# A recommendation tower on one core: each gathered group of embeddings is transposed in two pieces of 256 batch columns, the first one unit ahead of the second

## What is computed

```python
e = jnp.stack([tbl_0[ids[:, 0]], ..., tbl_39[ids[:, 39]]], axis=1)        # (512, 40, 32)
z = jnp.einsum('bpd,pde,bpe->bp', e[:, iidx, :], bilinear_matrices, e[:, jidx, :])   # (512, 780)
h = jnp.concatenate([z, dense_ctx], axis=1)                                # + 16 dense
h = jnp.maximum(h @ W_top1 + b_top1, 0.0)                                  # 796 -> 512
h = jnp.maximum(h @ W_top2 + b_top2, 0.0)                                  # 512 -> 256
y = h @ W_top3                                                             # 256 -> 1
```

## Time and profile before

| | us |
|---|---|
| median of 3 runs | 174.76 |
| lowest and highest of them | 174.19, 174.95 |
| the profiled execution, whole | 174.02 |
| its span in the profile | 172.2 |
| TensorE busy | 166.6 (97%) |
| VectorE busy | 145.4 (84%) |
| GpSimd busy | 115.1 (67%) |
| ScalarE busy | 43.6 (25%) |

### The profile page before, as it was taken

The page is one execution under the profiler, slowest core; times in us unless marked ns, Lnnn a source line. Parts: engine busy times, 40 slices in busy tenths (PEclk is TensorE's granted clock), DMA queues, the critical chain, the costliest instruction groups (busy, mean ns, idle before and its releaser), DMA issues.

```text
span 172.2 us, 4016 instructions
## 1 busy us (share of the span) xinstructions
PE 166.6 (97%) x1710; PEld 54.0 (31%) x1710; DVE 145.4 (84%) x144; ACT 43.6 (25%) x58; POOL 115.1 (67%) x119
## 2 busy tenths in 40 slices
PE   6999899999999999999999999999999999999993
PEld 2344344313333323332233333323233232232330
DVE  1799899889899998998999998999999999892600
ACT  2389994040101211102111201112100121110503
POOL 3777777777777777777777777777799995112000
PEclk9999999999999999999999999999999999999999
DMA  5999156986998720000006610001001650000000
GB/s 133 370 404 382 30 151 195 314 260 203 317 371 264 227 62 11 15 15 16 11 13 182 188 42 15 15 11 19 11 6 47 154 168 4 2 0 4 0 0 0
DMA packets 12699, 19.95 MB, mean 116 GB/s; under 512 B 3829, under 2 KB 6777, under 8 KB 12553
## 3 DMA queue, kind: packets, MB, share of 16 engines
q1 hardware_dynamic: 9144, 18.03, 31.9%
q0 software_dynamic: 3072, 1.58, 5.1%
q10 hardware_dynamic: 464, 0.09, 0.3%
HBM read 11.82 MB, written 0.00 MB: 69 GB/s over the span
## 4 chain that ended last, share of the span: by engine, by line
PE 85%; ACT 4%; DMA 4%; issue 2%; DVE 1%; SPq 1%
PE y_ps L559 33%; PE z_ps L630 27%; PE t_ps L530 11%; PE y_ps L530 7%; DMA table<-hot_tables 4%; PE y_ps L573 3%; PE t_ps L573 3%; ACT plane L414 2%; PE z_ps L573 1%; DVE prod L513 1%; ACT z_t L424 1%; SPq L356 1%; ACT xt L433 0%; ACT hot_id L471 0%; ACT xt L434 0%
## 5 line engine op out<-in xcount | busy, mean ns | idle before, releaser
L513 DVE TENSOR_TENSOR prod<-y_ps,xt 128x1024 f32<-128x1024 f32 x98 | 114.8, 1219 | 8.0 <-PE y_ps L559 3.5
L339 POOL DMA_INDIRECT x_rows<-rows,row x96 | 92.1, 960 | 29.2 <-issue 29.0
L559 PE MATMUL y_ps<-xt,m_sb 32*128 32x512 f32 x392 | 59.5, 640 | 0.0
L630 PE MATMUL z_ps<-prod,sel 128*32 128x512 f32 x392 | 52.2, 604 | 0.6 <-issue 0.4
L530 PE MATMUL t_ps<-z_t,table 128*32 128x256 f32 x352 | 27.1, 379 | 0.0
L488 DVE TENSOR_SCALAR hot<-hot_id,number 128x2048 bf16<-128x2048 int16 x34 | 22.8, 746 | 4.6 <-DMA hot_id<-hot_ids 4.1
L559 PEld LDWEIGHTS y_ps<-xt,m_sb 32*128 32x128 f32 x392 | 17.8, 182 | 22.6 <-DVE prod L513 13.4
L530 PEld LDWEIGHTS t_ps<-z_t,table 128*32 128x32 f32 x352 | 11.4, 110 | 26.3 <-issue 26.3
L630 PEld LDWEIGHTS z_ps<-prod,sel 128*32 128x32 f32 x392 | 7.8, 108 | 37.4 <-DVE prod L513 22.3
L573 PE MATMUL y_ps<-hot,plane 128*32 128x512 bf16 x200 | 15.1, 379 | 0.7 <-ACT plane L414 0.7
L347 POOL TENSOR_TENSOR hot_id<-x_rows,hot_id 128x512 f32<-128x512 f32 x6 | 7.6, 1272 | 9.5 <-ACT x_rows L457 9.5
(11 more groups left out here) (39 smaller groups left out, 62.3 us busy)
## 6 DMA issues: line engine op xcount, KB each, us to landing
xt<-xt SPq DMA_DIRECT2D x18, 192.0 KB, 2.5
xt<-xt SPq DMA_DIRECT2D x17, 128.0 KB, 2.4
hot_id<-hot_ids SPq DMA_DIRECT2D x4, 512.0 KB, 6.2
xt<-xt SPq DMA_DIRECT2D x32, 64.0 KB, 2.0
x_rows<-rows,row POOLq DMA_INDIRECT x96, 2.3
table<-hot_tables SPq DMA_DIRECT2D x2, 640.0 KB, 8.9
table<-w SPq DMA_DIRECT2D x1, 1280.0 KB
table<-hot_tables SPq DMA_DIRECT2D x2, 512.0 KB, 5.4
```

Of the source, the lines that this page charges most:

```text
L339: pool.indirect_dma_start(out=x_rows[:, g, c, :], out_offset=None, in_=rows, in_offset=bass.IndirectOffsetOnAxis(ap=row[:, n:n + 1], axis= ...
L513: nc.vector.tensor_tensor(prod[:, k % PROD_UNITS, 2 * half:2 * half + 2, :], y_ps[:, 2 * slot:2 * slot + 2, :], partners[half], ALU.mult). ...
L559: last = nc.tensor.matmul(y_ps[:, 2 * slot + place(t, u, s) % 2, :], m_sb[rows, k, :], xt[rows, moving(t, u, s), :], start=True, stop=True)
L630: last = nc.tensor.matmul(z_ps[s * DIM:(s + 1) * DIM, :], window, prod[:, k % PROD_UNITS, place(*UNIT[k], s), :], start=first, stop=(k == ...
```

## The change

The one transposition of a gathered group becomes two, of chunks 0 to 7 (columns 0 to 255) and chunks 8 to 15 (columns 256 to 511). `AFTER["turn"]` now has a unit for each piece. The first group's two pieces stand side by side ahead of unit 1; the others have the second piece where the whole turn stood, and the first piece ahead of the unit before. The wait for the gather stands ahead of the first piece, and is for all 16 chunks as before. Waits on `turned` count two for each group.

```diff
+TURN_PIECES = 2
...
-    "turn": [1, 8, 17, 23, 31, 39],
+    "turn": [(1, 1), (7, 8), (16, 17), (22, 23), (30, 31), (38, 39)],
...
-            engine.wait_ge(turned, GATHER_POS.index(t) + 1)
+            engine.wait_ge(turned, TURN_PIECES * (GATHER_POS.index(t) + 1))
...
-                            act.wait_ge(turned, part_free[b])
+                            act.wait_ge(turned, TURN_PIECES * part_free[b])
...
-                for g in [g for g, before in enumerate(AFTER["turn"]) if before == k]:
+                for g, piece in [(g, n) for g, units in enumerate(AFTER["turn"]) for n in range(TURN_PIECES) if units[n] == k]:
                     t = GATHER_POS[g]
-                    dve.wait_ge(gathered[g], 16 * CHUNKS)
-                    nc.vector.transpose(xt[:, t, :], x_rows[:, g, :, :].rearrange("p c d -> p (c d)")).then_inc(turned, 1)
+                    if piece == 0:
+                        dve.wait_ge(gathered[g], 16 * CHUNKS)
+                    part = slice(piece * CHUNKS // TURN_PIECES, (piece + 1) * CHUNKS // TURN_PIECES)
+                    nc.vector.transpose(xt[:, t, part.start * DIM:part.stop * DIM],
+                                        x_rows[:, g, part, :].rearrange("p c d -> p (c d)")).then_inc(turned, 1)
```

## The result

The changed kernel takes 177.34 us in the median of 6 runs, beside 174.78 of the kernel before: a ratio of 1.0132, 95% interval 1.0098 to 1.0165. The forecast was 176.8 us, range 175.5 to 178.0. The profiled execution took 177.31 us, with a span of 175.5, 3.3 more than before. Ratios here come from the executions of both kernels with the slow ones left out, and aren't quotients of the medians (which give 1.0146 here); where the two differ enough to matter, both are given.

What follows compares the result with a forecast made beforehand. TensorE was taken to bound the kernel, with VectorE's turns holding it up. A loss of 2.38 us at units 7 and 8 less 0.4 won elsewhere gave +2.0, so 176.8 us on the 174.76 median; range 175.5 to 178.0.

Steps and rivals of the forecast that it cites:

- What bounds the kernel: TensorE is busy 97% of the span; VectorE matters only where it holds TensorE up, about 0.46 us a turn.
- The gather isn't there one unit early: Group 4's gather lands at about 50.1 us, but the first piece ahead of unit 7 could start at 47.53.
- The working by steps: At units 7 to 10, the first piece's wait delays products and matmuls until unit 10 starts 2.38 us late.
- the sum: 2.38 us lost at units 7 and 8, less 0.4 won at the last four turns: +2.0 us.
- rival B: TensorE pauses 1.6 us in unit 8 and its clock falls: 2.9 us more, 179.7 us; chance 0.04.
- three signs that I had named for a wrong prediction: VectorE doesn't idle ahead of unit 7, a piece costs far from 440 ns, or matmuls behind the pause are slow.
- Unit 9's second half: It waits for unit 8's first product, which ends at 54.46, and starts at 54.51, 0.26 us late.
- The other four turns: Turns ahead of units 17, 23, 31 and 39: two pieces win 0.10 us each, -0.4 us together.
- The 0.05 us that goes free: Lateness of a product behind a turn that TensorE doesn't feel, some 0.05 us, counted against the pieces' cost.
- Rival A: Group 4's gather lands in time, at 46.0, so VectorE doesn't wait: -0.6 us, 174.2 us; chance 0.10.
- Rival C: A piece costs as much as a whole turn, 703 ns: about +2.5 us over the forecast, 179.3 us; chance 0.04.

Runs made afterwards that it cites:

- the kernel with the busy pause: The changed kernel with extra, overwritten matmuls filling TensorE's pause ahead of the second half of unit 8: 176.46 us, ratio 1.0123.
- the repeat: The changed kernel timed again, unedited, beside the kernel before: 177.47 us, ratio 1.0132.

## Why the prediction was right, and where its sizes were off

**What bounds the kernel**, and that a turn costs TensorE some 0.46 us: right. Small pieces, which fit into the spare time, take 0.40 of it away in each of four turns; from unit 7 to unit 48 that trace is 1.6 us shorter, and 2.15 with all five. The medians moved by more, 2.2 and 2.75 us. The kernel with only the loads moved shows the same surplus, some 0.5 us, over its trace, so part of it is probably that the traced execution of the kernel before was one of its better ones.

**The gather isn't there one unit early**: right, by the idle VectorE of 2.73 us (2.5 forecast) and by the kernel with only the wait moved. That SP's loads are the cause holds for about 3 us of the lateness; the other 1.2 have no cause that a run shows.

**The working by steps**, for the profiled executions (+3.3 where the sum gave +2.0):
- The first piece started at 50.35, not 50.12, and half of unit 8 at 51.96 (51.75 forecast): +0.2.
- Unit 9 starts at 56.09. With 2.50 us behind 51.96 it would have been 54.46: 1.6 us of slow clock, which I had kept out of the sum as **rival B with a chance of 0.04**. This is the term that was mis-sized. It came together with the forecast's mechanism, in ten of twelve executions. One of the three signs that I had named for a wrong prediction came true with it: the matmuls behind the pause are slow (1.73 and 1.94 us). Unit 10 starts at 58.59 and not near 57.0. My argument was that the longest pause before was 0.54 us and that work went on around it; no row showed how long a pause the clock bears, and I took that silence for a low chance. Its price of 2.9 us was too high: 1.6 in the trace, 1.4 net of what it covered, 1.0 between medians. That price came from the 14 first matmuls at 0.42 us each. The profile gives a granted clock of 1.00 for them too, so that they ran at the 1.2 GHz level was read from their length alone.
- Unit 9's second half, forecast 0.26 late, wasn't: the slow stretch covered it. With the clock kept up it is 0.24 late (1.38 us for 1.14, in the kernel with the busy pause). From 54.63 to 58.59, unit 10 is 3.96 late; 2.38 + 0.2 + 1.6 - 0.26 = 3.9.
- The other four turns gave back 0.66 us (3.95 late at unit 17, 3.29 at unit 48), not 0.4. The piece itself was right: 428 ns beside 439, and 0.36 and 0.46 us from start to start beside 0.36 and 0.48. The 0.05 us that goes free was counted once, but it goes free in each of the two units: 0.82 - 0.44 - 0.10 is 0.28 lost, and the matmuls of units 23 and 24 take 1.18 and 1.38 us, 0.28 over twice 1.14.

The medians differ by 2.6 us, beside 2.0 forecast, and that the two are so close is partly luck. The forecast added 0.74 us, by which the traced execution of the kernel before stood under its median. The changed kernel's traced execution (177.31) stands at its median (177.34), so those 0.74 us weren't there, and they made up for half of the slow clock. The two executions at full clock, 175.41 and 175.58 us, lie 1.2 us and more under the forecast; one of them is below its range.

**Rival A** (gather in time) was priced wrong. At -0.6 it left out its own consequence: the prediction called the later gathers close and had them in time because of the delay at unit 8. Without that delay an early piece waits for its own gather, group 7's in one trace (1.17 us) and group 8's in another (0.87). The kernel with the loads behind the gather came to 0.9996, not 0.995. Of the kernels with two pieces only the one with shorter waits (a semaphore for each piece) is faster than before.

**Rival C** is out: 428 ns for 256 columns, 297 for 128, 703 for 512.

## What to carry to other kernels

When an instruction is moved forward, move its wait in thought first: look in the trace for when the data landed, not for when the work was done, and for what stands between the new place and the old. Work that is cut into pieces to fit into another engine's spare time needs a wait that is cut too; here the pieces lost 1.3% with one wait for all the data and won 0.5% (two pieces) or 1.4% (four) with a wait each. Four pieces under one wait weren't tried, so how much of the 1.4% is the size and how much the waits isn't shown. Give a repair its control in the old kernel: moving the loads alone won 0.3%. A stall of TensorE is to be priced twice, for its length and for the clock behind it, here 1.8 and 1.6 us.

## What was unexpected of the hardware

Pauses of TensorE of 1.81 us, and of 2.24 in the repeat's trace, both of them behind about 1 us in which only half of a unit's matmuls ran, were followed by some 3 us at a granted clock of 0.50. One execution in six of each series kept 1.00 or 0.998, with a pause that no trace shows. With work in the pause, down to 0.34 us of idle time, the clock stayed in five of five. The gather's last chunk landed more than 6 us behind its issue at about 43.7 while the DMA engines were some 100% busy, where the median of all 96 is 2.3 us. With SP's loads held back and the DMA engines 6% to 12% busy from 44.0 to 47.4 us, it landed at 47.44. Its landing moved between the kernels' traces: pieces that waited for it started at 50.35, 50.50, 50.58, 50.85 and 50.99 us.
